# Accumulating two gathered slots in one matmul, and half of the key and value bias on TensorE, in a sparse graph attention kernel

## The reference

```python
q = (x @ Wq + bq).reshape(n, H, C)
k = (x @ Wk + bk).reshape(n, H, C)
v = (x @ Wv + bv).reshape(n, H, C)
attn = jnp.einsum('nhc,mhc->hnm', q, k) / np.float32(np.sqrt(C))
neg = jnp.where(mask[None], -jnp.inf, attn)
m = jnp.max(neg, axis=-1, keepdims=True)
...
denom = jnp.sum(e, axis=-1, keepdims=True)
alpha = e / jnp.where(denom == 0.0, 1.0, denom)
out = jnp.einsum('hnm,mhc->hnc', alpha, v)
...
x_r = x @ Ws + bs
beta = jax.nn.sigmoid(jnp.concatenate([out, x_r, out - x_r], axis=-1) @ Wb)
return beta * x_r + (1.0 - beta) * out
...
x = _layernorm(x + _L0_gnn_ref(x, adj, ...), axis=-1)
```

## Time and profile before

| quantity | value |
|---|---|
| median of 3 runs | 2172.78 us (2172.32 to 2172.80) |
| the profiled execution, its own time | 2167.49 us |
| its span | 2165.6 us, 1.9 us less |
| busy PE matmul, PE weight load | 1175.3 us, 707.2 us |
| busy VectorE, ScalarE, GpSimd | 1315.7 us, 841.0 us, 1119.0 us |
| mean granted TensorE clock | 0.68 of full speed |

### The profile page before, as it was taken

The page is one execution under the profiler, slowest core; times in us unless marked ns, Lnnn a source line. Parts: engine busy times, 40 slices in busy tenths (PEclk is TensorE's granted clock), DMA queues, the critical chain, the costliest instruction groups (busy, mean ns, idle before and its releaser), DMA issues.

```text
span 2165.6 us, 20121 instructions
## 1 busy us (share of the span) xinstructions
PE 1175.3 (54%) x4636; PEld 707.2 (33%) x4696; DVE 1315.7 (61%) x3427; ACT 841.0 (39%) x1595; POOL 1119.0 (52%) x1711
## 2 busy tenths in 40 slices
PE   6303545746646564556457665666477655551454
PEld 5101323424324332334324333343243332240233
DVE  5548776855856485356655565367466745781466
ACT  2304342324633254244443454355456733330112
POOL 4542656455266556665455447545655354557261
PEclk9556666657677576676676777677677766565566
DMA  8826955647576566475476566567677655324120
GB/s 316 337 61 240 268 175 193 237 164 267 192 244 225 190 229 236 167 255 211 158 287 219 208 235 249 198 233 279 212 267 284 221 213 209 97 63 106 54 83 22
DMA packets 130037, 438.70 MB, mean 203 GB/s; under 512 B 26567, under 2 KB 61198, under 8 KB 97150
## 3 DMA queue, kind: packets, MB, share of 16 engines
q1 hardware_dynamic: 76510, 297.15, 37.3%
q0 software_dynamic: 52832, 136.07, 20.5%
q10 hardware_dynamic: 576, 4.19, 0.5%
HBM read 417.93 MB, written 19.44 MB: 202 GB/s over the span
## 4 chain that ended last, share of the span: by engine, by line
DVE 32%; issue 22%; another core or an unknown queue 14%; DVEq 12%; PE 10%; ACT 7%; DMA 1%; ACTq 1%; POOL 0%; SPq 0%; POOLq 0%
DVE s_raw L1229 5%; DVEq L1277 4%; DVE s_kv L1227 4%; DVE s_wtop L1276 4%; ACT s_mask L1004 3%; PE s_ps_w L810 3%; DVE s_kv L1253 2%; PE s_acc L982 2%; DVE s_top L1324 2%; DVEq L1430 2%; DVE s_d_max L1441 1%; DVEq L1331 1%; ACT s_diag L1021 1%; DVE s_wtop L1270 1%
## 5 line engine op out<-in xcount | busy, mean ns | idle before, releaser
L781 POOL DMA_INDIRECT s_kv<-kv_rows,s_rec_in x1023 | 971.8, 950 | 825.1 <-PE s_acc L982 340.3
L810 PE MATMUL s_ps_w<-s_mask,s_bit_w 128*128 128x512 bf16 x1003 | 370.8, 517 | 306.1 <-ACT s_mask L1004 170.0
L1004 ACT ACTIVATE s_mask<-s_adj_in 128x2048 bf16<-128x2048 f32 x252 | 478.4, 1900 | 148.8 <-remote 61.0
L982 PE MATMUL s_acc<-s_kv,ident 128*128 128x128 f32 x2032 | 350.4, 341 | 240.7 <-issue 159.6
L982 PEld LDWEIGHTS s_acc<-s_kv,ident 128*128 128x128 f32 x2032 | 334.7, 255 | 266.0 <-issue 167.7
L810 PEld LDWEIGHTS s_ps_w<-s_mask,s_bit_w 128*128 128x128 bf16 x1008 | 109.1, 119 | 517.9 <-issue 263.5
L1229 DVE TENSOR_REDUCE s_raw<-s_kv 128x48 f32<-128x1536 f32 (+15 forms) x76 | 147.1, 1935 | 12.2 <-issue 6.8
L1253 DVE TENSOR_TENSOR s_kv<-s_kv,s_ps_q 128x1536 f32<-128x1536 f32 (+15 forms) x76 | 146.8, 1931 | 8.8 <-ACT s_ps_q L1043 4.0
L1441 DVE TENSOR_REDUCE s_d_max<-s_ps_key 128x1 f32<-128x1024 f32 x32 | 39.2, 1225 | 185.5 <-remote 159.0
L1227 DVE TENSOR_TENSOR s_kv<-s_kv,s_ps_q 128x1536 f32<-128x1536 f32 (+15 forms) x76 | 147.1, 1936 | 4.4 <-ACT s_or L1035 2.2
L1276 DVE MAX8 s_wtop<-s_words 128x8 f32<-128x512 f32 x171 | 118.8, 695 | 33.4 <-issue 20.7
(11 more groups left out here) (282 smaller groups left out, 1578.8 us busy)
## 6 DMA issues: line engine op xcount, KB each, us to landing
s_adj_in<-in_adj SPq DMA_DIRECT2D x248, 1024.0 KB
s_kv<-kv_rows,s_rec_in POOLq DMA_INDIRECT x1023
kv_rows<-s_kv SPq DMA_DIRECT2D x16, 512.0 KB, 7.2
s_rec_in<-node_records SPq DMA_DIRECT2D x55, 106.0 KB
s_kv<-in_x_cols SPq DMA_DIRECT2D x4, 1024.0 KB, 8.8
s_adj_in<-in_adj ACTq DMA_DIRECT2D x4, 1024.0 KB
s_d_in<-in_x_cols SPq DMA_DIRECT2D x8, 512.0 KB
s_d_v<-kv_rows SPq DMA_DIRECT2D x8, 512.0 KB
```

Source lines behind the costliest of these rows:

```text
L781: nc.gpsimd.indirect_dma_start(out=kv[0:n, START[k] + s], out_offset=None, in_=kv_dram[:, :], in_offset=bass.IndirectOffsetOnAxis(ap=rec_i ...
L810: last = nc.tensor.matmul(w[:], bit_w[:, slab], mask[:, k % 2, s * WORD:(s + 1) * WORD], start=False, stop=(slab == SLABS - 1))
L982: last = nc.tensor.matmul(acc[:, c * D:(c + 1) * D], ident[:], kv[:, START[k] + s, D:2 * D], start=(s == 0), stop=(s == plain(k) - 1))
L1004: nc.scalar.activation(mask[:, q % 2], adj_in[:, q % ADJ_RING], ACT.Sign, accum_out=edges[:, t, h:h + 1]).then_inc(masked, 1)
```

## The change

There are two edits.

**Two slots in one matmul.** In tiles of one unit, PE's matmul takes two neighbouring slots at once and adds 128x256 values into the first 256 columns of `acc`, so that each half of the columns collects every other slot. With an odd number of slots, one matmul of one slot stands next to last. `attend` gets a reduction on VectorE that adds the two halves into `osum`, in 54 tiles. Tiles of several chunks keep a matmul for each slot. Both releases of a unit stay; the first one stands on the matmul that holds the slot of before, which in 27 of the 54 tiles is one slot later. The 673 slots of the tiles of one unit take 350 matmuls, and all units together 693 where there were 1016.

**Half of the table's bias on PE.** In the second half of each group, PE adds the bias itself: behind each of the two matmuls comes one with a single row (`ones` x `b_row`) that accumulates into the same columns, 32 in all. ScalarE copies these halves to the staging slot (L1146, `kv_copied`), and VectorE keeps the 16 additions of the first halves. SyncE waits for both. ScalarE's four masks of tile 1 are placed ahead of the copies of groups 2, 5, 8 and 9. VectorE takes two word steps ahead of each of its additions from group 11 on, where it took one ahead of each of twice as many.

```diff
+FIRST_MASKS = [2, 5, 8, 9]
...
+def acc_steps(k):
+    m = plain(k)
+    if n_chunks(UNITS[k][0]) > 1:
+        return [(s, 1) for s in range(m)]
+    if m % 2 == 0:
+        return [(s, 2) for s in range(0, m, 2)]
+    return [(s, 2) for s in range(0, m - 3, 2)] + [(m - 3, 1), (m - 2, 2)]
...
-                sp.wait_ge(kv_ready, 2 * (g + 1))
+                sp.wait_ge(kv_ready, g + 1)
+                sp.wait_ge(kv_copied, g + 1)
...
-                    need(pe, kv_ready, b + 1 - 4)
+                    need(pe, (kv_ready, kv_copied)[half], g - 1)
                     for j in range(2):
                         k = g * GROUP + 2 * half + j
-                        last = nc.tensor.matmul(ps_kv[b % 4][:, j * 2 * D:(j + 1) * 2 * D], xT[:, k * P:(k + 1) * P],
-                                                w_all[:, 0:2 * D], start=True, stop=True)
+                        one = ps_kv[b % 4][:, j * 2 * D:(j + 1) * 2 * D]
+                        last = nc.tensor.matmul(one, xT[:, k * P:(k + 1) * P], w_all[:, 0:2 * D], start=True,
+                                                stop=(half == 0))
+                        if half:
+                            last = nc.tensor.matmul(one, ones[:], b_row[0:1, 0:2 * D], start=False, stop=True)
...
-                for s in range(plain(k)):
-                    if k in FOLD_UNITS and s == plain(k) - 1:
+                for s, n in acc_steps(k):
+                    ends = s + n == plain(k)
+                    if k in FOLD_UNITS and ends:
...
-                    last = nc.tensor.matmul(acc[:, c * D:(c + 1) * D], ident[:], kv[:, START[k] + s, D:2 * D],
-                                            start=(s == 0), stop=(s == plain(k) - 1))
-                    if s in (half(k) - 1, plain(k) - 1):
+                    last = nc.tensor.matmul(acc[:, c * D:(c + n) * D], ident[:], kv[:, START[k] + s:START[k] + s + n, D:2 * D],
+                                            start=(s == 0), stop=ends)
+                    if s <= half(k) - 1 < s + n or ends:
                         last.then_inc(summed, 1)
...
-            mask_tile(1)
+            for g in range(GROUPS):
+                if g in FIRST_MASKS:
+                    mask_part(1, FIRST_MASKS.index(g))
+                need(act, kv_stored[g % STAGES], 16 * (g // STAGES))
+                act.wait_ge(kv_summed, 2 * g + 2)
+                nc.scalar.copy(kv_stage[:, g % STAGES, 2:4], ps_kv[(2 * g + 1) % 4].rearrange("p (j c) -> p j c", j=2)
+                               ).then_inc(kv_copied, 1)
...
+                else:
+                    nc.vector.tensor_reduce(osum[:], acc[:, 0:2 * D].rearrange("p (n c) -> p c n", n=2), AX, ALU.add)
+                    sums = osum[:]
...
```

More of the change, by code:

```diff
@@ L478, in sparse_tiles @@
         kv_ready = sem("kv_ready")
+        kv_copied = sem("kv_copied")
         pad_stored = sem("pad_stored")
@@ L939, in _ @@
             turn_rows(1)
-            pe.wait_ge(kv_ready, 2 * GROUPS)
+            pe.wait_ge(kv_ready, GROUPS)
+            pe.wait_ge(kv_copied, GROUPS)
             project_qr(1)
@@ L1608, in add_kv_bias @@
                 need(dve, kv_stored[g % STAGES], 16 * (g // STAGES))
[L1609 to L1617, removed]
+                if g >= FIRST_WORDS:
+                    dve.drain()
+                    take_words(1, 2 * (g - FIRST_WORDS), 2 * (g - FIRST_WORDS) + 2)
+                dve.wait_ge(kv_summed, 2 * g + 1)
+                nc.vector.tensor_tensor(kv_stage[:, g % STAGES, 0:2], ps_kv[2 * g % 4].rearrange("p (j c) -> p j c", j=2),
+                                        b_kv.unsqueeze(1).to_broadcast([P, 2, 2 * D]), ALU.add).then_inc(kv_ready, 1)
             dve.wait_ge(bias_spread, 1)
```

## The result

The changed kernel is slower. Its median is 2193.22 us against 2172.79 us before (10 runs each); the ratio is 1.0096, with a 95% interval of 1.0072 to 1.0121, so about +21 us, between 16 and 26. Two of the ten executions of the changed kernel, at 2212 and 2216 us, lie over 1.5% above its fastest and are left out of the ratio. The prediction was 2186 us in a range of 2160 to 2206, +13 us.

The account below looks back on a forecast made before the run. No engine is always busy; TensorE, then VectorE, sets the table stage, and a late start is lost whole. Table +17, streaming -2, delivery -14, reductions +9, release +3 give +13 us on 2172.8: 2186 us, range 2160 to 2206.

Parts of the forecast that it names:

- the first rival: Table stage: one-row bias passes cost no more than others, so decoding starts 5 us late; 2174 us in all; chance 0.13.
- rival 2: Units: halving the matmul count relieves PE's slow stretches more, -45 us in place of -14, giving 2155 us; chance 0.20.
- rival 4: All 54 added reductions on VectorE are exposed and the start is 17 us late: 2198 to 2203 us; chance 0.10.
- The table term (+17): Table stage: one-row bias matmuls make a group 3.38 us instead of 1.73; decoding starts at 79.0 instead of 62.02.
- The clock rival (3): TensorE's clock falls to 1.2 GHz within the table stage: start 60 us later, 2229 to 2245 us; chance 0.05.
- The reductions (+9): VectorE's 54 added reductions, 22 us of work, 21 to 24 of them exposed: +9 us, bounds 0 and +23.
- Delivery (-14): Accumulation: fewer matmuls shorten the catch-ups after PE's slowly arriving instructions: 14 us saved, bounds 0 and 35.
- streaming: Accumulation: passes twice as wide save at most 14 us of PE time; 2 us on the path, bounds 0 and 5.
- half the passes shorten the catch-up behind it: After the slow stretch in tile 11's accumulation, catch-up falls from about 3.6 to 1.8 us; eight such catch-ups assumed.
- mostly nobody gains from a faster end there: In slow stretches of one-unit tiles' accumulation, finishing passes earlier mostly helps no engine; tile 11's 15.76 us VectorE wait is the example.
- The release (+3): First `summed` a slot later in 27 tiles delays POOL's gather-slot release 0.2 to 0.4 us: +3 us, bounds 0 and +8.

## Why the prediction was right, and where it was not

**Its direction and size held**: +13 forecast, +21 measured, with the first rival's price (+5 for the table), the relief of rival 2 and the full exposure of rival 4 all refuted by runs. The 8 us between are -1.5 in the table, +1 in the reductions and the rest in what pairing gives back. The range of 46 us was wide enough to hold the sum without any relief from delivery too (2200 us), so that the result lies in it says nothing for that term.

**The table term (+17) is shown.** The group of 3.38 us measured 3.37, and decoding started 15.5 us late. The 1.5 us between arose ahead of the packing, and 1 us of it in the first two groups. PE began 0.3 us earlier (12.63 against 12.97). The first group came out 1.4 us dearer (4.93 against 3.54), much as taken. The second was 1.1 us dearer (3.37 against 2.26) and not 1.65, because it had been partly at the low clock before: full clock was granted from 17.6 us there and from 16.0 in the changed kernel. That the loss goes to the end undiminished is shown by the chain, whose "issue" stretch ends 15.4 us later, and by four kernels on the quick chips whose medians follow the start of decoding.

**Rival 1 was wrong for its stated reason.** The Trainium skill (TensorE: Matmul & The Clock Gate, section "Why this matters for your kernels") has a single matmul over 32 rows take the time of one over 128. Where matmuls of one row alternate with full ones, the runs show a difference: 0.31 us a pass with one row, 0.216 with the same columns over 128 rows, in kernels that differ in the bias matmul alone.

**The clock rival (3) was right in part.** It had the clock fall within the stage. What the traces show is a rise that comes late in some executions, by up to 11 us of low clock, and costs up to 6 us more (decoding at 83.2 against 77.5). I had looked only at how busy the engine is, and had read the 1.00 of the earlier trace rows as the clock of the whole stage, though the first 4.6 us of it, to 17.6, were at 1.2 GHz. That the one-row matmuls make the rise late rests on four traces and stays unproven.

**The reductions (+9) measured +10 and +13** (3 to 16, and 9 to 17). About half of 22.9 us is exposed, as taken.

**Delivery (-14) is the term that failed.** The slow arrival of passes is real and did shrink: "issue" ahead of the accumulation's matmuls fell from 159.6 to 92.0 us. But the measured 21 less 15.5 for the table and 10 for the reductions leaves -4 or so for delivery, streaming and release together, where I had -13. The pairs alone on another chip of this kind, +6 less the same 10, leave -4 as well. With the intervals of the two runs the first -4 lies between -13 and +4, so the sum alone hardly excludes my number; the waits speak more clearly.

The step that failed reads "half the passes shorten the catch-up behind it", taken for eight waits. In the earlier trace rows the last pass did end VectorE's wait (892.99, and 893.01 for the update). But of the twelve long waits at this place only five, with 49.4 of 105.9 us, ended with a matmul even before the change, and I made tile 11's the model of all. In the changed kernel the passes of the same tile are done at 876.4 and the release comes at 908.05, and all ten long waits are of this sort. Tile 11's is set by POOL's run: before, the run ends at 882.7 and the first, late update is recorded at 889.65, 6.9 us behind; now it ends at 901.1 and the update comes at 907.91, 6.8 us behind. Eight of the ten have POOL idle for 2.1 to 6.9 us when their update is recorded. PE's instructions and the news were both held until then, so what half the passes save in the catch-up turns into waiting. Shortly before it the prediction says "mostly nobody gains from a faster end there"; that was right, and the term should have been near its lower bound, 0; the sum would then have been 27 with the same other terms, and 22.5 with the table at 15.5 and the release at nothing.

**The release (+3)** can't be told apart from nothing: pairs without reductions are at -2 us, between -5 and 0, on the chip where no pass is late.

**What stays open**: why VectorE, PE and ScalarE are held during POOL's runs on one kind of chip and not on the other, and whether pairing slots brings anything at all there.

## What to carry to other kernels

Look first at which engine sets a stage, group by group, before moving work off another: PE set this one until 38 us, and only behind that was VectorE late; moved there alone, and over all rows, the bias gains 6 us on one chip, and on another the interval just takes in no change. A bias by a matmul of one row isn't cheap among full matmuls: write it over all rows. And when a wait ends together with the work it waits for, look whether the other waits of its kind do so too, and find what held both; halving the work ends nothing if the news of it is what was late.

## What the runs showed of the hardware that I had not expected

- One-row matmuls add 0.10 us to each of their own passes, to the last full pass ahead and to the first behind, at 256 and at 512 columns. Pairs alternating with full ones run at 0.31 us a pass instead of 0.216.
- With one-row matmuls in the first groups, full clock (2.4 GHz) came at 16.0, 20.4, 22.0 and 28.4 us; without, at 15.5 to 17.6 in ten traces. That the one thing makes the other is not shown.
- The same kernel takes 1636 us on one chip and 2172 on another, with a table stage equal to 0.5 us. Where the traces differ is in times when POOL issues gathers without a pause: there, on the slower chip, the other engines get on slowly, and the raising of a semaphore by a finished accumulation was recorded 32 us late, 7 us after POOL's run had ended.
